# Token order inside a 512-token tile: partition p holds tokens 4p to 4p+3 instead of p, p+128, p+256, p+384

## What is computed

```
u   = rmsnorm(layernorm(x)) * norm1_w
z, xs, B, C, dt_raw = split(u @ in_proj_w.T)      # 256, 64, 64, 256, 128 columns
dt  = softplus(dt_raw @ dt_proj_w.T + dt_proj_b)
h_t = exp(dt_t * A) * h_(t-1) + (dt_t * xs_t) * B_t   # along the sequence, 256 channels x 32 states
y_t = sum over states of h_t * C_t
y   = (y + xs * D_param) * silu(z)                # the "gated y"
h   = layernorm(x) + y @ out_proj_w.T
x   = x + h + (silu(hn @ gate_w.T) * (hn @ up_w.T)) @ down_w.T      # hn = rmsnorm(h) * norm2_w
xn  = layernorm(x)
out = x + fwht(silu(xn @ W1.T) * (xn @ W3.T)) @ W2.T
```

## Time and profile before

| what | value |
|---|---|
| median of 3 runs | 1129.17 us (1128.63 to 1129.44) |
| the profiled execution's own time | 1129.54 us |
| its span in the profile | 1127.5 us |
| PE busy | 1017.4 us (90%) |
| DVE busy | 1006.2 us (89%) |
| ACT busy | 629.5 us (56%) |
| POOL busy | 868.9 us (77%) |
| hardware DMA queue of SP, share of 16 DMA engines | 82.7% |

### The profile page before, as it was taken

The page is one execution under the profiler, slowest core; times in us unless marked ns, Lnnn a source line. Parts: engine busy times, 40 slices in busy tenths (PEclk is TensorE's granted clock), DMA queues, the critical chain, the costliest instruction groups (busy, mean ns, idle before and its releaser), DMA issues.

```text
span 1127.5 us, 13622 instructions
## 1 busy us (share of the span) xinstructions
PE 1017.4 (90%) x3816; PEld 525.6 (47%) x3816; DVE 1006.2 (89%) x1133; ACT 629.5 (56%) x1267; POOL 868.9 (77%) x444
## 2 busy tenths in 40 slices
PE   3486689899999999999999999999999989898998
PEld 1222134446454554436453554446453543446777
DVE  4599999999999999999999999999999999997342
ACT  4455675548755675548655675548655554443220
POOL 2589898788988798888988798888988888785100
PEclk9686699999999999999999999999999999999999
DMA  6998899997999899997989798997999798870000
GB/s 229 220 210 203 195 234 246 234 222 183 234 215 223 176 231 197 226 206 191 236 205 219 176 233 201 225 205 187 234 209 208 174 228 182 191 162 19 1 1 19
DMA packets 124602, 213.93 MB, mean 190 GB/s; under 512 B 18608, under 2 KB 27760, under 8 KB 124400
## 3 DMA queue, kind: packets, MB, share of 16 engines
q1 hardware_dynamic: 122800, 209.36, 82.7%
q0 software_dynamic: 1008, 3.67, 0.9%
q10 hardware_dynamic: 720, 0.04, 0.0%
HBM read 185.99 MB, written 12.06 MB: 176 GB/s over the span
## 4 chain that ended last, share of the span: by engine, by line
PE 66%; DVE 14%; issue 8%; ACT 7%; DMA 3%; SPq 1%; POOL 1%; DVEq 0%; POOLq 0%; ACTq 0%
PE p_r L581 17%; PE p_r L570 10%; DVE h_s L1110 9%; PE p_r L587 9%; PE p_y L536 7%; PE p_dt L525 6%; PE p_r L576 5%; PE p_r L556 3%; DVE bt_s L1092 3%; ACT p_dt L742 2%; PE p_dt L681 2%; PE p_r L681 2%; ACT tok L791 2%; DMA bt_s<-dx_rows 2%; PE p_r L691 1%
## 5 line engine op out<-in xcount | busy, mean ns | idle before, releaser
L1374 POOL TENSOR_TENSOR h_s<-h_s,c_s 128x1024 f32<-128x1024 f32 x255 | 556.0, 2183 | 125.2 <-DVE h_s L1110 123.0
L742 ACT ACTIVATE p_dt<-p_dt,an_s 128x512 f32<-128x512 f32 x372 | 241.4, 660 | 247.6 <-PE p_dt L525 247.4
L1110 DVE TENSOR_TENSOR_SCAN h_s<-p_dt,carry,bt_s 128x512 f32<-128x512 f32 x256 | 319.2, 1270 | 6.6 <-ACT p_dt L742 6.4
L1110 DVE TENSOR_TENSOR_SCAN h_s<-p_dt,bt_s 128x512 f32<-128x512 f32 x256 | 302.6, 1211 | 13.1 <-ACT p_dt L742 13.0
L525 PE MATMUL p_dt<-kdt,pick_s 128*128 128x512 f32 x372 | 231.4, 635 | 65.9 <-DVE h_s L1110 53.5
L1349 POOL TENSOR_TENSOR bt_s<-bt_s,b_s 128x1024 f32<-128x1024 f32 x101 | 238.9, 2365 | 17.7 <-DMA bt_s<-dx_rows 12.7
L581 PE MATMUL p_r<-nT,w_s 128*128 128x512 f32 x448 | 204.7, 597 | 0.7
L1092 DVE TENSOR_TENSOR bt_s<-bt_s,p_b 128x1024 f32<-128x1024 f32 x155 | 186.3, 1202 | 9.0 <-DMA bt_s<-dx_rows 9.0
L525 PEld LDWEIGHTS p_dt<-kdt,pick_s 128*128 128x128 f32 x372 | 72.6, 198 | 200.5 <-DVE h_s L1110 131.5
L570 PE MATMUL p_r<-nT,gu_s 128*128 128x512 f32 x308 | 143.5, 599 | 3.8 <-ACT nT L944 3.8
L536 PE MATMUL p_y<-h_s,ysel_s 128*32 128x512 f32 x1024 | 143.9, 636 | 1.8 <-POOL h_s L1374 1.8
(11 more groups left out here) (152 smaller groups left out, 931.5 us busy)
## 6 DMA issues: line engine op xcount, KB each, us to landing
bt_s<-dx_rows SPq DMA_DIRECT2D x512, 256.0 KB, 5.9
dtr_s<-dt_rows SPq DMA_DIRECT2D x224, 128.0 KB, 6.5
dtr_s<-dt_rows SPq DMA_DIRECT2D x112, 64.0 KB, 6.0
kdt<-st_dt SPq DMA_DIRECT2D x36, 128.0 KB, 5.6
tok<-in_x SPq DMA_DIRECT2D x8, 512.0 KB, 7.4
xo<-in_x SPq DMA_DIRECT2D x8, 512.0 KB, 4.0
xr_s<-xb_s SPq DMA_DIRECT2D x64, 64.0 KB, 5.9
b_s<-xb_s SPq DMA_DIRECT2D x64, 64.0 KB, 4.3
```

The source lines that it names most:

```text
L742: A(p_dt[DT_BANK[u]][:, :], dt_in, ACT.Exp, scale=an_s[:, c:c + 1]).then_inc(a_dA, 1)
L1110: V.tensor_tensor_scan(h_s[:, u % 8, 1:T + 1], p_dt[DT_BANK[u]][:, :], bt_s[:, u % 16, :], carry[:, u:u + 1] if par else 0.0, ALU.mult, AL ...
L1374: G.tensor_tensor(h_s[:, two, 0:T], h_s[:, two, 1:T + 1], c_s[:, h, :].unsqueeze(1).broadcast_to([P, 2, T]), ALU.mult)\
```

## The change

All loads of x and all stores of out take the rows of a tile as "(p s)" instead of "(s p)": partition p then holds the four consecutive tokens 4p to 4p+3, 4 KB in a row in DRAM, where it held four separate rows of 1 KB. The transposed blocks of tok now hold tokens s, s+4, s+8 and so on; to keep the columns of uT_s in the order of time, the copy from the bank to uT_s (L881) writes with a step of four elements (16 bytes). In the same way out_proj takes every fourth column of zs_s as its 128 weights (L565, L666), and the halves of the last tile's gate (L1267, L1270) are no longer the first and second 256 tokens but the tokens with s in {0, 1} and s in {2, 3}. The number of instructions, their sizes and the semaphores stay as they are.

```
+        def tokens(a, s, n=1):
+            return a.rearrange("p (q s) -> p s q", s=SUB)[:, s:s + n, :]
         def rows(dram, t):
-            return dram[bass.ds(t * T, T), :].rearrange("(s p) d -> p s d", p=P)
+            return dram[bass.ds(t * T, T), :].rearrange("(p s) d -> p s d", s=SUB)
...
-                dst = out_t[bass.ds(LAST * T + N2 * a, N2), :].rearrange("(s p) d -> p s d", p=P)
+                dst = rows(out_t, LAST)[:, 2 * a:2 * a + 2, :]
...
-                    ins = nc.tensor.matmul(ps[:, D * (j // 2):D * (j // 2) + D], zs_s[:, c, P * s:P * s + P],
+                    ins = nc.tensor.matmul(ps[:, D * (j // 2):D * (j // 2) + D], tokens(zs_s[:, c, :], s),
...
-                                A(uT_s[:, other, k, :], ring[BANK["uT", k]][:, :], ACT.Copy,
+                                src = ring[BANK["uT", k]][:, :].rearrange("p (s q) -> p s q", s=SUB)
+                                A(tokens(uT_s[:, other, k, :], 0, SUB), src, ACT.Copy,
                                   scale=par_s[:, k:k + 1]).then_inc(a_uT, 1)
...
-                    V.scalar_tensor_tensor(out=p_y[:, half(a)], in0=xr_s[:, LAST % 2, 1, half(a)], scalar=par_s[:, 7:8],
-                                           in1=p_y[:, half(a)], op0=ALU.mult, op1=ALU.add).then_inc(t_yf, 1)
+                    V.scalar_tensor_tensor(out=tokens(p_y[:, :], 2 * a, 2), in0=tokens(xr_s[:, LAST % 2, 1, :], 2 * a, 2),
+                                           scalar=par_s[:, 7:8], in1=tokens(p_y[:, :], 2 * a, 2), op0=ALU.mult, op1=ALU.add).then_inc(t_yf, 1)
                     dve.wait_ge(t_yf, a + 1)
-                    V.scalar_tensor_tensor(out=zs_s[:, 1, half(a)], in0=zs_s[:, 1, half(a)], scalar=0.5,
-                                           in1=p_y[:, half(a)], op0=ALU.mult, op1=ALU.mult).then_inc(t_yz, 1)
+                    V.scalar_tensor_tensor(out=tokens(zs_s[:, 1, :], 2 * a, 2), in0=tokens(zs_s[:, 1, :], 2 * a, 2), scalar=0.5,
+                                           in1=tokens(p_y[:, :], 2 * a, 2), op0=ALU.mult, op1=ALU.mult).then_inc(t_yz, 1)
```

## The result

The changed kernel took 1132.70 us as the median of 8 runs (1131.20 to 1133.37), the kernel before, run beside it, 1128.84. The ratio is 1.0028 with a 95% interval of 1.0017 to 1.0039: **slower by 0.3%, some 3 us**. The forecast was 1128.5, no difference. The time lies in the stated range, but on the side that got 28% of the chances, and the interval does not hold 1. (A ratio in this document is worked out from the single runs of both kernels and is not the quotient of the two medians: here that would be 1.0034.)

A forecast was written before the change was run, and what follows sets the result against it. PE and DVE arithmetic was taken to bound the kernel, with transfers mostly hidden. First load -0.5, last store -0.05 and other transfers -0.1 gave -0.65 us, from a median of 1129.17 to 1128.5 us; range 1127.0 to 1135.0.

The forecast's parts named there:

- What bounds the kernel: Whole kernel: bound by arithmetic on PE (busy 90%) and DVE (89%) handing over to each other, transfers mostly hidden.
- Transfers: Interior loads and stores: fewer, larger packets save 0.12 us of an engine per load, nearly all hidden; -0.1 us in all.
- The first load: First load of x, on the chain: fewer packets may shorten its slow ramp; bounds 0 and -1.05, taken as -0.5 us.
- The three zeros for the step of 16 bytes: Copy to uT_s, out_proj's weight loads and the tail's gate: the step was taken to cost 0 us each.
- the ends that I had set by doubling: Upper costs if elements take twice as long: copy +414 ns, weight load 297 ns, record +81 ns, gate instruction +0.25 us.
- Rival B: Copies on the chain +2.5 us, first tile's pair 0.6, tail's gate +0.5: ACT and DVE pay, 1132.1 us; chance 0.12.
- Rival C: out_proj's weight loads: PE pays about 1.05 us per tile, 7.3 for seven, plus 0.65 in the tail; 1136.5 us; chance 0.12.
- D: Copies, gate and out_proj: Rival B and Rival C together, 1140.1 us, or 1136 with the latter at half; chance 0.06.

The follow-up runs named there:

- e10: Kernel before with the copy to uT_s writing in 16-byte steps in tiles 2 to 7 only; 1128.89 us, ratio 1.0003.
- e1: Kernel before with only the row order of the loads of x and stores of out changed; 1128.79 us, ratio 1.0003.
- e5: Changed kernel, but the copy to uT_s writes contiguously and reads its PSUM bank with a step of 128 elements; 1130.56 us, ratio 1.0011.
- e6: Changed kernel, but the transposes write every fourth column of the PSUM bank and the copy is contiguous; 1129.21 us, ratio 0.9999.
- e9: Kernel before with the copy to uT_s writing in 16-byte steps in tiles 0 and 1 only; 1131.40 us, ratio 1.0016.
- e3: Kernel before with the step only in out_proj's weight loads inside the tiles, not in the tail; 1129.63 us, ratio 1.0004.
- e12: The changed kernel measured again, unaltered, against the kernel before on the same chip; 1131.47 us, ratio 1.0020.
- e4: Kernel before with the step only in the last tile's gate and the 16 weight loads behind it; 1130.80 us, ratio 1.0013.
- e13: Kernel before with two unused DVE additions ahead of the last tile's gate as a pause, no steps; 1128.92 us, ratio 1.0002.
- e14: Kernel before with four unused matmuls filling TensorE's gaps around the tail; 1127.29 us, ratio 0.9995.
- e15: Kernel before with the step only in the tail's gate and weight loads, plus four unused matmuls in TensorE's gaps; 1128.00 us, ratio 0.9988.
- e16: Changed kernel with four unused matmuls filling TensorE's gaps around the tail; 1130.10 us, ratio 1.0007.

## Why the prediction was wrong

**What bounds the kernel**: right. PE and DVE hold the middle, and 760 us of it took no notice of ten copies that are 0.5 us longer each (760.07 us in e10).

**Transfers**: right in size. I took -0.1 us for the interior and e1 shows nothing. The packets under 2 KB fell by 8704 and not by some 12,000: 16 loads of 512 and the 512 of the last stores. POOL's stores were no packets of 1 KB before: 1008 packets for 3.67 MB, the very row that I took a price from.

**The first load**: -0.5 us was too much. It landed in 3.80 us after, in place of 3.96; over the profiles it took 3.5 to 4.1 us in the new order and 3.7 to 4.0 in the old, with means of 3.71 and 3.85. By these means a quarter of the packets took some 0.14 us off it, and most of the slow ramp has another cause, which no run isolates.

**The three zeros for the step of 16 bytes**: this is the step that failed. "I take 0: ACT asks for only 1.2 elements per ns, a step changes no count of elements" was an argument about the engine's rate, and the cost is in the access to SBUF: the same copy with the step on its read side took 683 ns again (e5). Measured against the ends that I had set by doubling:

- the copy +495 ns, over its upper end of 414;
- a weight load +135 ns, over its upper end of 107, but its record only +16, against an end of 81;
- the gate's instructions +194 and +209 ns, under the end of 250.

Doubling was a guess and no bound from above: the column part of the copy became 2.2 times and that of a load 2.3 times as long (414 + 495 against 414 ns, 107 + 135 against 107). The rule that I weighed against the zeros (the Trainium skill, Advanced Engine Details and Errata, SBUF Cachelines) held in its direction, and should have had more than the 0.30 that B, C and D got together: each operation of this case with one f32 per 16 bytes of SBUF became slower, by 40% (678 / 484) to 72% (1178 / 683). For the gate no run separates SBUF from PSUM. The same page's rule for PSUM, that any pattern with gaps slows matmuls significantly (PSUM Cachelines), is not borne out by e6: its transposes write every fourth f32 at an unchanged 273 ns. No run has another kind of matmul write with gaps.

**Rival B** named the mechanism, ACT and DVE pay for the step, and its 1132.1 us is close to the measured 1132.7, partly by luck. Its place was wrong. It put 2.5 us on the three pairs of copies that the chain ran through the earlier trace rows. Of these only the first seems to have cost anything, with the pair of the first tile and perhaps that of tile 2 (e9, e10); the pairs at 407 and 660 us (e10's expectation miscounts them as tiles 3 and 5) had another path as long as the one through ACT, and when ACT got slower the chain went by DVE there. **Rival C** had PE pay 1.05 us per tile; e3 has 0.4 us for all seven by its ratio, not told from zero, and the stretch from 217 to 977 us agrees. That the tail's clock would move by another 1.2 us in the profiled run no case foresaw.

**The sum as the runs show it**: copies at the start 1 to 2 us, tail 0.64 us by durations, weights about 0.4, transfers nothing that can be told. That is 2.0 to 3.0 us, against 2.3 (e12) and 3.2 us (first measurement). The difference may be the tail's clock. What stays open is whether the tail's steps make the clock come back later, as five of six profiles suggest and e4 and e13 don't. The failed step itself is not in doubt: three terms were put at nothing, and each of the three accesses measured longer, the copy's most.

## What to carry to other kernels

A change that trades the packets of a transfer for a step in on-chip accesses has to be priced at the accesses: one f32 per 16 bytes cost 40 to 72% here, on ACT's write to SBUF, on the weight loads and on DVE's gate (in SBUF and PSUM together), while the same reordering done in PSUM, by the transposes or by the reading side of the copy, was free. Where an operation lies on the chain of waits in one profile, ask for the second path before multiplying its extra time by its count; in this kernel the fill of the pipeline is where such a cost seems to have stayed. And look at the granted clock behind every gap of TensorE on the chain.

## What was not expected of the hardware

A write to SBUF with a step of 16 bytes takes ACT 2.2 times the column part of a contiguous one (414 + 495 against 414 ns for 512 columns). PSUM showed no such price for ACT's reads (step 512 bytes, 683 ns both ways) nor for TensorE's writes (step 16 bytes, 273 ns both ways). Weight loads of 325 ns ran at a pace of 232 ns per record. Four unused matmuls in gaps of TensorE kept the granted clock at 1.00 (e14, e15, e16) and made the next 16 records 1.7 us faster than in the kernel before (3.72 against 5.41).
